# A two-layer graph network on one core: the first stage written anew in unrolled blocks of 128 rows

## What is computed

```python
    h = jnp.maximum(_layernorm(x, axis=-1), 0.0)
    x = x + _L0_gnn_ref(h, src, dst, ...)      # attention, then a feed-forward part
    h = jnp.maximum(_layernorm(x, axis=-1), 0.0)
    x = x + _L1_gnn_ref(h, src, dst, edge_type_8, ...)
# _L0: the part that the first stage of the kernel computes
        h = layernorm(triplet_h, ln_attn_g, ln_attn_b)
        qkv = (h @ Wqkv + bqkv).reshape(n, 3, H, DH)
        q = qkv[:, 0] * SCALE
        k = qkv[:, 1]
        v = qkv[:, 2]
# then a softmax of q[src].k[dst] over the edges of a node, a sum of v[src],
# a layernorm, a 256 -> 1024 -> 256 feed-forward part with gelu, and x + y
# _L1: W = comp x basis (8 relation matrices of 256x256); h_all = h @ W for all
# relations; a sum of h_all[src, type] per destination; + h @ loop_w; gelu; layernorm
```

## Time and profile before

| | us |
|---|---|
| median of 3 runs | 1698.16 (1694.78 to 1698.62) |
| the profiled execution, its own time | 1690.69 |
| span of its trace, first to last instruction | 1688.6 |
| stage one, up to the first instruction of stage two | 205.4 |
| stage two | 205 to 732 |
| stage three | 733 to 1154 |
| stage four | 1155.7 to 1688.6 |

### The profile page before, as it was taken

The page is one execution under the profiler, slowest core; times in us unless marked ns, Lnnn a source line. Parts: engine busy times, 40 slices in busy tenths (PEclk is TensorE's granted clock), DMA queues, the critical chain, the costliest instruction groups (busy, mean ns, idle before and its releaser), DMA issues. The chain is left out here.

```text
span 1688.6 us, 25178 instructions
## 1 busy us (share of the span) xinstructions
PE 1229.1 (73%) x4992; PEld 832.7 (49%) x4992; DVE 973.0 (58%) x3071; ACT 388.5 (23%) x991; POOL 887.1 (53%) x934
## 2 busy tenths in 40 slices
PE   1567187888787878839999999993666776666773
PEld 0233066666665666626565655642444554444552
DVE  4455478888887888765455544231355454455554
ACT  1355133333332333223323232220000000000000
POOL 1730077777777777722122021014777777777771
PEclk9778699999999999969999999996787778788776
DMA  3533488888888888823212111123444444444441
GB/s 115 94 119 118 167 258 255 260 260 256 258 260 256 255 259 260 256 89 107 107 49 97 44 77 62 60 86 101 122 133 130 130 127 127 130 130 130 127 127 46
DMA packets 135072, 255.21 MB, mean 151 GB/s; under 512 B 38008, under 2 KB 84283, under 8 KB 131922
## 3 DMA queue, kind: packets, MB, share of 16 engines
q0 software_dynamic: 50176, 154.19, 30.7%
q1 hardware_dynamic: 84871, 100.76, 18.0%
HBM read 193.31 MB, written 61.57 MB: 151 GB/s over the span
## 5 line engine op out<-in xcount | busy, mean ns | idle before, releaser
L791 POOL DMA_INDIRECT arena<-qv_tab,arena x392 | 392.8, 1002 | 144.5 <-issue 126.9
L1393 POOL DMA_INDIRECT arena<-h_all,arena x392 | 376.3, 960 | 145.4 <-issue 104.5
L1462 PE MATMUL ps<-arena 128*128 128x256 f32 x784 | 275.1, 498 | 164.3 <-DMA arena<-h_all,arena 129.1
L1462 PEld LDWEIGHTS ps<-arena 128*128 128x128 f32 x784 | 180.5, 246 | 248.8 <-DMA arena<-h_all,arena 178.2
L895 PE MATMUL ps<-arena 128*128 128x264 f32 x800 | 234.1, 417 | 49.6 <-DVE arena L974 49.2
L884 PE MATMUL ps<-arena 128*128 128x264 bf16 x1188 | 174.7, 284 | 43.9 <-DVE arena L963 43.1
L986 DVE TENSOR_TENSOR arena<-arena,ps 128x512 f32<-128x512 f32 x196 | 134.3, 685 | 91.7 <-DMA arena<-qv_tab,arena 80.2
L895 PEld LDWEIGHTS ps<-arena 128*128 128x128 f32 x800 | 139.3, 194 | 96.8 <-DVE arena L974 57.1
L884 PEld LDWEIGHTS ps<-arena 128*128 128x128 bf16 x1188 | 140.5, 146 | 93.1 <-DVE arena L963 78.3
L1202 PE MATMUL ps<-wrel,arena 128*125 128x512 f32 x400 | 176.7, 595 | 5.3 <-ACT arena L1142 5.3
L1100 POOL COPY hs<-arena 125x256 f32 (+1 forms) x25 | 9.9, 396 | 271.2 <-ACT arena L1137 271.2
(11 more groups left out here) (171 smaller groups left out, 1499.0 us busy)
## 6 DMA issues: line engine op xcount, KB each, us to landing
h_all<-arena SPq DMA_DIRECT2D x25, 1000.0 KB
arena<-dst SPq DMA_DIRECT2D x51, 256.0 KB, 4.9
arena<-k_tab SPq DMA_DIRECT2D x50, 198.0 KB
att<-arena SPq DMA_DIRECT2D x51, 132.0 KB
rel<-arena SPq DMA_DIRECT2D x50, 128.0 KB
arena<-qv_tab,arena POOLq DMA_INDIRECT x392, 4.4
arena<-h_all,arena POOLq DMA_INDIRECT x392, 2.9
qv_tab<-arena SPq DMA_DIRECT2D x25, 250.0 KB
```

The source lines that it names most:

```text
L791: pool.indirect_dma_start(out=rowbuf[:, u * T + t, 0:2 * D], out_offset=None, in_=qv_tab, in_offset=bass.IndirectOffsetOnAxis(ap=idx[:, u, ...
L1393: pool.indirect_dma_start(out=rowbuf[:, u * T + t, :], out_offset=None, in_=h_all, in_offset=bass.IndirectOffsetOnAxis(ap=idx[:, u, t:t + ...
L1462: last = nc.tensor.matmul(ps[:, 6 + u, 0:D], ind[:, u, t, :], rowbuf[:, u * T + t, :], start=(t == 0), stop=False)
```

## The change

Blocks have P = 128 rows, of which the last block has 53 real ones (LASTP); the tables in DRAM grow to 3200 rows. This holds in stages three and four too, whose code is otherwise as it was. In stage one the loops are written out. `x` comes in six pieces, five of them ahead of most other loads. The weights and the first norm's gain and bias are issued on ACT's queue. The gain is multiplied into the weights (`wqs`) and the bias goes through eight PE instructions into `bq`; `features` becomes a plain copy, one instruction per block. The two subtractions of the key parts move from DVE to POOL, which does one step of the relation matrices between them and the last 11 of its 35 steps behind the last block. The statistics of the next chunk now stand behind the take of the chunk's first block, and the window arithmetic stands in blocks 1 and 11. `qvst` and `kst` have six slots. The edge lists are loaded in 15 pieces between the stores.

```diff
...
-P = 125
-NBLK = N // P
+P = 128
+NBLK = -(-N // P)
+NP = NBLK * P
+LASTP = N - (NBLK - 1) * P
...
+    h_all = nc.dram_tensor("h_all", (NP * R, D), FP32).ap()
...
+            NST, NH, NK, NR = 6, 10, 4, 3
+            hn = cut([NH, D])
+            hT = cut([2, 2, P])
+            qvst = cut([NST, 2, D])
...
+            CHUNKS = [(0, 2), (2, 5)] + [(c, c + 5) for c in range(5, NBLK, 5)]
...
-                sp.dma_start(xs_v[:, 0:CH, :], x_v[:, 0:CH, :]).then_inc(s_x0, 16)
...
-                sp.dma_start(xs_v[:, CH:NBLK, :], x_v[:, CH:NBLK, :]).then_inc(s_x, 16)
+
+                def load_x(c):
+                    lo, hi = CHUNKS[c]
+                    if hi == NBLK:
+                        sp.dma_start(xs_v[0:LASTP, NBLK - 1, :], x[N - LASTP:N, :]).then_inc(s_x[c], 16)
+                        hi -= 1
+                    sp.dma_start(xs_v[:, lo:hi, :], x_v[:, lo:hi, :]).then_inc(s_x[c], 16)
+
+                load_x(0)
+                load_x(1)
+                sp.wait_ge(padded, 5)
+                sp.dma_start(rows[0:FULL, :], dst[0:FULL * GE].rearrange("(g e) -> g e", g=FULL)).then_inc(s_rows, 16)
+                sp.dma_start(rows[FULL:G, 0:REST], dst[FULL * GE:E].rearrange("(g e) -> g e", g=1)).then_inc(s_rows, 16)
+                load_x(2)
+                load_x(3)
                 sp.dma_start(cmpb[:, :], comp.rearrange("r b -> (r b)").partition_broadcast(128)).then_inc(s_basis, 16)
                 sp.dma_start(base, basis.rearrange("b (k p) o -> p b k o", p=128)).then_inc(s_basis, 16)
...
+                load_x(4)
+                load_x(5)
...
-                with sp.Fori(0, NCH) as i:
-                    sp.dma_start(att[bass.ds(i * CH * P, CH * P), :].rearrange("(b p) d -> p b d", p=P), zero).then_inc(z_out, 16)
-                    for j in range(CH):
-                        b = i * CH + j
-                        sp.wait_ge(qkv_taken, 2 * b + 12)
-                        sp.dma_start(qv_tab[bass.ds(b * P, P), :], qvst[:, j, :]).then_inc(stored[j], 16)
-                        sp.wait_ge(kl_ready, b + 1)
-                        sp.dma_start(k_tab[bass.ds(b * P, P), :], kst[:, j, :, :].rearrange("p c d -> p (c d)")).then_inc(stored[j], 16)
+                for b in range(NBLK):
+                    j = b % NST
+                    sp.wait_ge(qkv_taken, 2 * b + 1)
+                    sp.dma_start(qv_tab[b * P:(b + 1) * P, :], qvst[:, j, :, :].rearrange("p c d -> p (c d)")).then_inc(stored[j], 16)
+                    sp.wait_ge(kl_ready, b + 1)
+                    sp.dma_start(k_tab[b * P:(b + 1) * P, :], kst[:, j, :, :].rearrange("p c d -> p (c d)")).then_inc(stored[j], 16)
...
+                    if b % CH == 4:
+                        c = b - 4
+                        sp.dma_start(att[c * P:(c + CH) * P, :].rearrange("(b p) d -> p b d", p=P),
+                                     zero[:, 0:1, :].broadcast_to([P, CH, AW])).then_inc(z_out, 16)
+                    if 2 <= b < 17:
+                        edge_piece(b - 2)
...
-                for j in range(CH):
-                    sp.wait_ge(stored[j], 32 * NCH + 32)
+                for j in range(NST):
+                    sp.wait_ge(stored[j], 32 * len(range(j, NBLK, NST)))
...
+                def rest_of_keys(b):
...
+                    nc.gpsimd.tensor_tensor(r1[:, b % NR, :], kf[:, b % NK, :], kst[:, b % NST, 0, 0:D], ALU.subtract).then_inc(r1_ready, 1)
+
+                def last_of_keys(b):
...
+                    nc.gpsimd.tensor_tensor(kst[:, b % NST, 2, 0:D], r1[:, b % NR, :], kst[:, b % NST, 1, 0:D],
+                                            ALU.subtract).then_inc(kl_ready, 1)
+
+                relations = relation_steps()
+                for b in range(NBLK + 1):
+                    if b == 2:
+                        pool.wait_ge(s_basis, 32)
+                    if b < NBLK:
+                        rest_of_keys(b)
+                    if b >= 2:
+                        next(relations, None)
+                    if b >= 1:
+                        last_of_keys(b - 1)
+                for _ in relations:
+                    pass
                 pool.wait_ge(nmax_in, 1)
                 nc.gpsimd.partition_all_reduce(nmr[:, :], nmx[:, :], 128, RMAX).then_inc(nmax_back, 1)
...
+                act.dma_start(wq, Wqkv.rearrange("(k p) (c d) -> p k c d", p=128, d=D)).then_inc(s_w, 16)
+                for n, a in enumerate((ga, ba)):
+                    act.dma_start(cols[:, n, :], a.rearrange("(k p) -> p k", p=128),
+                                  allow_slow_non_contiguous=True).then_inc(s_w, 16)
+                act.dma_start(bq.rearrange("p c d -> p (c d)"), bqkv.partition_broadcast(128)).then_inc(s_w, 16)
...
-                def features(i, j):
-                    act.wait_ge(hT_in_psum, 2 * (i * CH + j) + 3)
-                    for k in range(2):
-                        nc.scalar.activation(hT[:, j, k, :], ps[:, j % 2, k * P:k * P + P], ACT.Identity,
-                                             bias=cols[:, 1, k:k + 1], scale=cols[:, 0, k:k + 1]).then_inc(hT_ready, 1)
...
+                def features(b):
+                    act.wait_ge(hT_in_psum, b + 1)
+                    if b >= 2:
+                        act.wait_ge(qkv_ready, b - 1)
+                    nc.scalar.activation(hT[:, b % 2, :, :], ps[:, b % 2, 0:2 * P].rearrange("p (k n) -> p k n", k=2),
+                                         ACT.Copy).then_inc(hT_ready, 1)
...
+                for b in range(NBLK + 1):
+                    c, p = b // CH + 2, b % CH
+                    more = b < NBLK - CH
+                    if b + 1 < NBLK:
+                        if not (more and p == 4):
+                            features(b + 1)
+                    if more and p == 0:
+                        root_x(c)
+                    if more and 1 <= p <= 3:
+                        relu(c, [CHUNKS[c][0] + n for n in ((0, 1), (2, 3), (4,))[p - 1]])
+                    if more and p == 4:
+                        root_h(c)
+                    if b < NBLK:
+                        first_of_keys(b)
+                        norms(b)
+                    if more and p == 4:
+                        features(b + 1)
+                    if b >= 1:
+                        second_of_keys(b - 1)
...
+                pe.wait_ge(s_w, 64)
+                pe.wait_ge(bcol_ready, 1)
+                for half in range(2):
+                    for k in range(2):
+                        bank, n, w = parts(wq, k)[half]
+                        last = nc.tensor.matmul(ps[:, bank, 0:n], bcol[:, k, :], w, start=(k == 0), stop=(k == 1))
+                last.then_inc(bias_psum, 1)
...
+                pe.wait_ge(wqs_ready, 2)
+                pe.wait_ge(bias_ready, 2)
+                for b in range(NBLK):
...
-                def chunk(i, last):
-
-                    if not last:
-                        dve.wait_ge(s_x, 16)
-                        x_stats(i + 1)
-                    for j in range(CH + 3):
-                        b = i * CH + j
-                        if j == 4 and not last:
-                            h_stats(i + 1, (4,))
-                            spread(i + 1, st6b, mvb, rsb)
-                        if j < CH:
-                            dve.wait_ge(qkv_ready, b + 1)
-                            dve.wait_ge(stored[j], 32 * i + 32)
-                            nc.vector.tensor_tensor(qvst[:, j, :], ps[0:P, 2 + j % 2, :], bq[:, 0:2 * D],
-                                                    ALU.add).then_inc(qkv_taken, 1)
-                            nc.vector.tensor_tensor(kf[:, j, :], ps[0:P, 4 + j % 2, 0:D], bq[:, 2 * D:3 * D],
-                                                    ALU.add).then_inc(qkv_taken, 1)
-                        if not last:
-                            if j == 0:
-                                x_scale(i + 1)
-                            if 2 <= j <= 3:
-                                h_stats(i + 1, ((0, 1), (2, 3))[j - 2])
-                        if 1 <= j <= CH:
-                            dve.wait_ge(kh_ready, b)
-                            nc.vector.tensor_tensor(r1[:, j - 1, :], kf[:, j - 1, :], kst[:, j - 1, 0, 0:D],
-                                                    ALU.subtract).then_inc(r1_ready, 1)
-                        if 3 <= j:
-                            dve.wait_ge(km_ready, b - 2)
-                            nc.vector.tensor_tensor(kst[:, j - 3, 2, 0:D], r1[:, j - 3, :], kst[:, j - 3, 1, 0:D],
-                                                    ALU.subtract).then_inc(kl_ready, 1)
...
+                dve.sem_inc(bcol_ready, 1)
+                h_stats(range(*CHUNKS[1]))
+                aggregate(1, st6b, mvb, rsb)
...
+                nc.vector.tensor_tensor(bq[:, 0::2, :], ps[:, 2, :].rearrange("p (c d) -> p c d", d=D), bq[:, 0::2, :],
+                                        ALU.add).then_inc(bias_ready, 1)
```

(26 more changed lines are left out.)

517 lines of the change are left out of this document (270 added, 247 removed).

## The result

The kernel after took 1646.79 us (median of 4 runs, 1644.67 to 1649.13), the kernel before 1697.08 us (4 runs). The ratio is 0.9705, interval 0.9686 to 0.9724: 50.3 us less, where 52 were forecast. The profiled execution of after took 1649.13 us, its span is 1647.3.

A forecast was written before the change was run, and what follows sets the result against it. Stage one was taken to be bound by its own stores (DMA share 0.33, 118 GB/s). Stage one -43, other stages -10 and last store +1 gave -52 us, so 1698.2 became 1646 us; range 1620 to 1668.

The forecast's parts named there:

- Transfers: Stage one's stores: with 128 rows a block's 0.600 MB takes 2.4 us, under 12 us per chunk, no longer setting the pace.
- Start: Stage one up to the end of the first projection: about 26 us against 30.7 before, weights taken to land at 10.
- Chunk: Five blocks of stage one with statistics: 22.5 us each, four of them 90, including a 2.2 us gap at the start.
- POOL becomes the pace: Rival, stage one: bfloat16 subtraction costs 1.55 us, a block about 5, chunk 25; +10 to +16, total 1659 us; chance 0.22.
- Better overlap: Rival, stage one: the new gap closes and the clock stays high, chunk 20.5 us; total 1632 us; chance 0.18.
- The +6: Stage one: 6 us added for window arithmetic inside blocks 1 and 11 and the first blocks at the low clock.
- Last four blocks: End of stage one's blocks, without statistics: takes and relation matrices on DVE, about 3.4 us each, 13.5 in all.
- Tail: Stage one behind the last projection: key parts 6.3, 11 relation steps 15.4, small steps 1.6, about 3 more; 26 us.
- Stage three: First load -4 us, wider PE instructions +2, end with its two 1 MB stores -8; together -10.
- Stages two and four: Paced by POOL's indirect transfers, which do not change: 0 us, with 3 either way; moving over 5 us would refute the forecast.
- The clock rival: Rival, stage one: two gaps per chunk keep TensorE at 1.2 GHz, chunk 35.5 us; total 1709 us; chance 0.04.
- The upper end: Stage one with every high guess (start 33, chunk 25, tail 29): 185 us, where 162 was forecast.

## Why the prediction was right

The time was forecast at 1646 and is 1646.8; the mechanism, store width, is shown from both sides. But the sum came out so well partly by luck, because errors cancelled. And one of its own signs of being wrong came: stage two moved by more than 5 us in the profiled pair.

- **Stage one in all**: -43 forecast, -39.5 measured.
- **Transfers**: right. 0.33 went (0.31 in the first chunk, at 93 GB/s, and 0.49 to 0.60 in the other three), the waits for `k_tab` went. The 0.586 MB of a block is right, though its three terms mix units of 1000 and 1024 bytes.
- **Start**, 26 us: measured 27.9. The weights were not the limit, nor the eight bias steps (4.66 us; 5.4 forecast), but DVE, held by POOL's steps of 1274 columns. I had priced that contention only inside the chunks. The bias steps were to begin at 13.4 us and began at 19.0; that it cost only 1.9 us is luck, since the first projection, priced at 5.4, took 2.75 and the bias steps 0.7 less. The eight instructions of 5.37 us in the earlier trace rows, from which both prices came, stand at a granted clock that reads 1.00 up to 31 us, so that the low clock was their reason is not shown.
- **Chunk**, 22.5: measured 22.4, 21.6, 22.9, 23.3, with the forecast gap at its start (2.40; 2.2) and the clock of 0.9 (0.89). The rival "POOL becomes the pace" falls: its subtraction took 0.67 us in either type where DVE left it alone, and no chunk reached 25. "Better overlap" falls too, with a gap of 2.40 us.
- **The +6** for window arithmetic and the low clock: too much. The four chunks together took 90.3 us, with the window arithmetic in them, and the projections had the full rate from the first one on (25.11 to 27.86, eight steps in 2.75 us). This is the mis-sized term on the good side: 5.7 us.
- **Last four blocks**, 13.5: 14.1 between the first takes.
- **Tail**, 26: about 33 from the last take. The 11 relation steps took 16.0 (15.4 forecast). Missing was the 5.7 us ahead of the reduction: the step "1.6 of small steps" took the reduction for a short one, since the trace of before showed it behind 83 us of idle time.
- **Stage three**: first load -3.6 (-4), end -9.3 (-8), what lies between +2.8, of which the wider forms of one line are 2.1 (63.0 + 41.9 instead of 61.6 + 41.2 us busy; +2): -10.1 (-10). Last store +1.4 (+1).
- **Stages two and four**: 0 ± 3 forecast; stage two differed by +6.5 us in the profiled pair, beyond the 5 that I had named as the limit, and by -3.3 on a chip where both ran; stage four by +1.9 and +0.9. Open for the first chip.
- **The clock rival** (1.2 GHz in the chunks) did not come near: 0.85 to 0.93 in the chunks. But the reason given against it, that the mean never fell to 0.8 in the old chunks, was wrong: it was 0.77 and 0.70 in the first two (49.9 to 87.2 and 87.2 to 112.4 us), 0.86 and 0.93 in the next two.
- **The upper end**: start 33, chunk 25 and tail 29 add up to 181.5, not 185. The measured 166.0 is far from either.

What the prediction did not see is its own lever: it listed the 15.4 us of POOL's tail and the 2.2 us gap as costs of the change and left them, and both were to be had for one line each.

## What to carry to other kernels

A DMA share that stood flat near a multiple of a sixteenth (0.33, a little over 5 of 16) while no engine was full was a matter of row counts here. Where you see one, try to split the store first (here in 112 and 13 rows), before rewriting anything; that alone gave nearly half of this gain. Work handed to an engine with idle time must also end in time: look at what stands behind the last block, since there every step is on the path. And an instruction that follows idle time shows only its duration; what comes ahead of it appears when the idle time is filled.

## What the runs showed of the hardware

- POOL stood still for 5.5 to 6.2 us between other work of its own and a reduction over partitions (nine reductions in eight profiled executions); where it had been idle for 68 us or more, the reduction followed DVE's last values within 0.2 to 0.3 us (four executions). What it does there no row names.
- DVE steps on two or three numbers per partition took 2.3 to 2.7 us instead of 0.17 beside POOL steps of 2.3 to 3.5 us, and 1.7 to 2.9 us in a second execution of the kernel after.
- The same 392 gathers of stage two spanned 511 to 520 us on the first chip (granted clock 0.98, 258 GB/s between 255 and 705 us in the kernel before) and 705 to 721 us on the others (0.81 and 182 GB/s between 255 and 905 us in the kernel before on one of them). There the longest waits of the kernel before between 255 and 905 us were of two kinds, where "remote" is a queue that the profile cannot name; on the first chip POOL's wait for L812 came to 3.7 us in all of stage two:

```profile
ACT arena L828 <- remote: 248.7, 45, 7.5
POOL arena L791 <- ACT arena L812: 189.5, 41, 5.8
```

The lower clock does not hold throughout on that chip: in stage three, where PE waits for little, both chips took 361.5 us of PE work in the same 379 us at a granted clock of 0.99 (760 to 1139 us on the first chip, 976 to 1355 on the other, kernel before). Whether the clock in stage two is cause or consequence of the longer waits was not tried. The gain of stage one in microseconds carried over, its ratio did not.
